# Key terms of three cross attentions made inside other stages, and two heads' keys loaded ahead of time

## What is computed

```python
q = (x @ Wq + bq).reshape(1, 1024, 16, 8)
k = (ctx_1024 @ Wk + bk).reshape(1, 6404, 16, 8)
v = (ctx_1024 @ Wv + bv).reshape(1, 6404, 16, 8)
attn = softmax(einsum('bthd,bshd->bhts', q, k) / sqrt(8), axis=-1)
out = einsum('bhts,bshd->bthd', attn, v).reshape(1, 1024, 128)
```

## Time and profile before

| | |
|---|---|
| Median of 3 runs | 4346.12 us (4341.44 to 4347.59) |
| Span of the profiled execution | 4349.1 us |
| TensorE busy | 3644.3 us, 84% |
| VectorE busy | 3405.6 us, 78% |
| ScalarE busy | 2821.1 us, 65% |
| GpSimd busy | 274.0 us, 6% |
| Score maxima on VectorE (L1666) | 2791.2 us in 2496 reductions |
| Exponentials on ScalarE (L1647) | 2452.8 us |

### The profile page before, as it was taken

The page is one execution under the profiler, slowest core; times in us unless marked ns, Lnnn a source line. Parts: engine busy times, 40 slices in busy tenths (PEclk is TensorE's granted clock), DMA queues, the critical chain, the costliest instruction groups (busy, mean ns, idle before and its releaser), DMA issues. The chain is left out here.

```text
span 4349.1 us, 85479 instructions
## 1 busy us (share of the span) xinstructions
PE 3644.3 (84%) x35064; PEld 1230.6 (28%) x35126; DVE 3405.6 (78%) x3306; ACT 2821.1 (65%) x4041; POOL 274.0 (6%) x199
## 2 busy tenths in 40 slices
PE   5774699999999747999999997399748999999995
PEld 2551222222222212222222222155312222222221
DVE  4323799999999328999999992499839999999982
ACT  0332288888888722888888886155415888888884
POOL 3001000000000010000000000244310000000000
PEclk9557599999999965999999999699857999999998
DMA  3003211111111031101111101100040111111100
GB/s 98 1 1 67 34 18 23 26 27 20 21 27 15 18 78 24 26 14 27 26 27 22 19 15 32 34 5 5 5 87 12 27 27 27 22 18 27 27 4 21
DMA packets 56289, 114.71 MB, mean 26 GB/s; under 512 B 10592, under 2 KB 46304, under 8 KB 50944
## 3 DMA queue, kind: packets, MB, share of 16 engines
q1 hardware_dynamic: 55936, 109.72, 14.1%
HBM read 84.08 MB, written 25.50 MB: 25 GB/s over the span
## 5 line engine op out<-in xcount | busy, mean ns | idle before, releaser
L1666 DVE TENSOR_REDUCE chunk_max<-max_scores 128x2 f32<-128x988 f32 (+1 forms) x2496 | 2791.2, 1179 | 193.4 <-PE max_scores L1549 158.2
L1647 ACT ACTIVATE probs<-scores 128x512 f32<-128x512 f32 (+1 forms) x3231 | 2452.8, 808 | 536.3 <-PE scores L1575 513.6
L1602 PE MATMUL values_sum<-probs,values 128*9 128x256 f32 x19584 | 1378.8, 384 | 26.7 <-DVE values_sum_s L1677 18.5
L1575 PE MATMUL scores<-queries,key_ring 49*128 49x512 bf16 x4800 | 1232.8, 386 | 50.9 <-ACT probs L1647 18.3
L1549 PE MATMUL max_scores<-key_ring,queries 48*128 48x494 bf16 (+1 forms) x4992 | 986.0, 393 | 157.6 <-DVE chunk_max L1666 113.1
L1602 PEld LDWEIGHTS values_sum<-probs,values 128*9 128x9 f32 x19584 | 376.8, 89 | 791.0 <-issue 569.2
L1575 PEld LDWEIGHTS scores<-queries,key_ring 49*128 49x128 bf16 x4800 | 308.1, 94 | 644.4 <-ACT probs L1647 542.3
L1549 PEld LDWEIGHTS max_scores<-key_ring,queries 48*128 48x128 bf16 x4992 | 241.0, 94 | 853.6 <-DVE chunk_max L1666 546.8
L1186 ACT ACTIVATE probs<-scores 128x512 f32<-128x512 f32 x256 | 138.5, 592 | 106.0 <-PE scores L1138 106.0
L1212 DVE TENSOR_REDUCE chunk_max<-max_scores 128x1024 f32 (+1 forms) x128 | 155.0, 1214 | 25.9 <-PE max_scores L1094 25.8
L1677 DVE COPY values_sum_s<-values_sum 128x256 f32<-128x256 f32 x48 | 20.0, 416 | 183.7 <-PE values_sum L1602 183.7
(11 more groups left out here) (183 smaller groups left out, 1742.5 us busy)
## 6 DMA issues: line engine op xcount, KB each, us to landing
key_ring<-k_parts SPq DMA_DIRECT2D x96, 300.2 KB
key_ring<-k_parts SPq DMA_DIRECT2D x96, 200.1 KB
k_parts<-k_part SPq DMA_DIRECT2D x108, 128.0 KB, 2.3
key_ring<-k_parts SPq DMA_DIRECT2D x96, 100.1 KB
o_whole<-values_sum_s SPq DMA_DIRECT2D x48, 128.0 KB, 7.0
queries<-q_parts SPq DMA_DIRECT2D x36, 128.0 KB
context<-in_ctx_t SPq DMA_DIRECT2D x1, 3202.0 KB, 17.2
q_parts<-q_part SPq DMA_DIRECT2D x12, 256.0 KB, 2.8
```

Of the source, the lines that this page charges most:

```text
L1575: return pe.matmul(sc[:, g % 3, :], keys(rows, h, P * t, P * (t + 1)), qb[rows, q], start=True, stop=True)
L1602: mm = pe.matmul(acc[32 * b:32 * b + WV, 0:QBLOCK], vb[rows, h, t, :], pr[rows, slot, QBLOCK * (b % 2):QBLOCK * (b % 2 + 1)], start=(t == ...
L1647: act.activation(pr[:, a % RING:a % RING + b - a, :], sc[:, a % 3:a % 3 + b - a, :], ACT.Exp)\
L1666: dve.tensor_reduce(mx[:, h % 2, c, :, j], mxb[:, w % 2, :, 0:width], AX.X, ALU.max)\
```

## The change

- `key_terms` is gone. The first cross attention's key terms are made in the first layer's value stage, now `project_values_and_keys`: before each of the first 13 value products stands a key product, with the same split and the same three slots. VectorE's sum over the context stands behind its key work.
- The key terms of the second and third cross attention are made in the tail of the one before (`ahead`): behind operation 1005 and every fourth after it TensorE makes one chunk's product into a bank of the score maxima; VectorE makes all three terms (four instructions a chunk) in the unused half of `queries`, with four slots, and SyncE stores them. Each cross attention has a `k_parts` of its own.
- The 12 fetches of query rows move to the end of `query_terms`, each group behind the store of its term.
- The keys of heads 0 and 1 are loaded ahead of `cross_attention`: beside `project_windowed` for the first, in a stage of their own (`load_first_keys`) behind the first cross attention for the second, and behind `clear_self_rows` of the self attention for the third (one ring place further, `base` = 1).
- The ones in the ring are filled once: 3072 columns by GpSimd and one row of each half from memory (`ones_row`, 9606 floats). What the self attention overwrites is filled again by GpSimd beside a layer norm.

```diff
--- before.py
+++ after.py
+def ring_keys(k, rows, h, base, lo=0, hi=M):
+    at = ((h + base) % KRING) * M
+    return k.key_ring[rows, at + lo:at + hi]
+
+def load_keys(k, sp, h, base, k_parts, loaded):
+    for half in range(2):
+        for p, run_length in enumerate(K_RUNS):
+            row = 64 * half + FIRST_ROW[p]
+            sp.dma_start(ring_keys(k, slice(row, row + HD * run_length), h, base),
+                         k_parts[h, 0:run_length].rearrange("p d n -> (p d) n")).then_inc(loaded, 16)
+
+def load_first_keys(k, layer, base, k_parts):
+    with ExitStack() as ctx:
+        block = ctx.enter_context(k.nc.Block())
+        @block.sync
+        def _(sp):
+            for h in range(2):
+                load_keys(k, sp, h, base, k_parts, k.first_keys[layer])
+
+def store_key_terms(sp, k_parts, part, c, slot, stored):
+    w = chunk_width(c)
+    for p in range(NPART):
+        sp.dma_start(k_parts[:, p, :, CHUNK * c:CHUNK * c + w], part[:, p, slot, 0:w]).then_inc(stored, 16)
+
-def project_values(k, xn, wv, vs, beside_vector):
+def project_values_and_keys(k, xn, wv, vs, wk, bk, k_parts, beside_vector):
...
+            def keys(c):
+                if c >= 4:
+                    pe.wait_ge(rest_ready, c - 3)
+                pe.matmul(kbank[c % 4][:, 0:chunk_width(c)], wk, k.ctx_t[:, CHUNK * c:CHUNK * c + chunk_width(c)],
+                          start=True, stop=True).then_inc(k_product, 1)
+
+            for g in range(NSEG):
+                if g < NCHUNK:
+                    keys(g)
+                values(g)
...
             for g in range(NSEG):
+                if g < NCHUNK:
+                    act.wait_ge(k_product, g + 1)
+                    if g >= 3:
+                        act.wait_ge(stored[g % 3], 16 * NPART * (g // 3))
+                    w = chunk_width(g)
+                    act.activation(part[:, 0, g % 3, 0:w], kbank[g % 4][:, 0:w], ACT.Identity, bias=bk).then_inc(high, 1)
                 act.wait_ge(projected, g + 1)
                 act.activation(vs[:, g, :], bank[g % 4][:], ACT.Copy).then_inc(copied, 1)
+                if g < NCHUNK:
+                    middle_part(g)
...
+            for c in range(NCHUNK):
+                dve.wait_ge(high, c + 1)
+                if c >= 3:
+                    dve.wait_ge(low, c - 2)
...
+                if c >= 1:
+                    low_part(c - 1)
+            low_part(NCHUNK - 1)
             beside_vector(dve)
...
-def project_windowed(k, w_o, o_pairs):
+def project_windowed(k, w_o, o_pairs, k_parts, ones_row):
...
+                pool.memset(k.key_ring[64 * half + 32:64 * half + 64, 0:KRING * N].bitcast(F32), PAIR_OF_ONES)\
+                    .then_inc(filled, 1)
...
+            sp.wait_ge(filled, 2)
+            for half in range(2):
+                row = 64 * half + KROWS
+                sp.dma_start(k.key_ring[row:row + 1, :].bitcast(F32), ones_row).then_inc(k.first_keys[0], 16)
+            for h in range(2):
+                load_keys(k, sp, h, 0, k_parts, k.first_keys[0])
...
@@ query_terms @@
             for p in range(NPART):
                 sp.wait_ge(stored[p], 16)
+                if rows_of is not None:
+                    for half in range(2):
+                        for r in range(K_RUNS[p]):
...
+            if rows_of is not None:
+                sp.wait_ge(fetched, 16 * 2 * NTERM)
...
-def key_terms(k, wk, bk, kb, qb, q_parts, k_parts):
...
+AHEAD_EVERY = 4
-def cross_attention(k, kb, qb, vb, k_parts, o_whole, wv):
+def cross_attention(k, layer, base, qb, vb, k_parts, o_whole, wv, ahead=None):
...
-            load_keys(0)
-            load_keys(1)
             max_rows(0)
...
+            if ahead is not None:
+                for c in range(NCHUNK):
+                    sp.wait_ge(next_low, c + 1)
+                    store_key_terms(sp, ahead[2], part, c, c % 4, next_stored[c % 4])
             store_values(H - 1)
...
+                if ahead is not None and n > tail_op and (n - tail_op) % AHEAD_EVERY == 1:
+                    next_key_product((n - tail_op) // AHEAD_EVERY)
...
+            def next_key_terms(c):
...
+                dve.wait_ge(next_product, c + 1)
+                if c >= 4:
+                    dve.wait_ge(next_stored[slot], 16 * NPART * (c // 4))
+                if bk is None:
+                    dve.tensor_copy(first, src).then_inc(next_high, 1)
...
             for h in range(H):
+                if h == H - 1 and ahead is not None:
+                    for c in range(NCHUNK):
+                        next_key_terms(c)
...
@@ program, attend @@
-                key_terms(k, k.w[prefix + w[1]], bk, kb, qb, q_parts, k_parts)
...
+            if layer == 0:
+                load_first_keys(k, 1, 0, k_parts[1])
             then()
...
             clear_self_rows(k, kb, qb)
+            load_first_keys(k, 2, 1, k_parts[2])
...
+            layer_norm(k, k.x[:], v["L3_xattn_ln2_g"], v["L3_xattn_ln2_b"], hn[:], t1[:], t2[:], beside=restore_ones(k))
```

More of the change, by code:

```diff
@@ L96, in __init__ @@
         self.steps = 0
+        self.first_keys = [ctx.enter_context(nc.semaphore(f"first_keys_{n}")) for n in range(3)]
     def name(self, text):
@@ L446, in _, with values @@
         def _(pe):
-            for g in range(NSEG):
+            def values(g):
                 if g >= 4:
@@ L466, in project_extra_values, with _ @@
+            low_part(NCHUNK - 1)
+            beside_vector(dve)
+        @block.sync
+        def _(sp):
+            for c in range(NCHUNK):
+                sp.wait_ge(high, c + 1)
+                sp.wait_ge(middle, c + 1)
+                sp.wait_ge(low, c + 1)
+                store_key_terms(sp, k_parts, part, c, c % 3, stored[c % 3])
+            for b in range(3):
+                sp.wait_ge(stored[b], 16 * NPART * len(range(b, NCHUNK, 3)))
 def project_extra_values(k, mem_tok, wv, vx):
@@ L798, in query_terms @@
         stored = [sem("stored") for _ in range(NPART)]
+        fetched = sem("fetched")
         block = open_phase(k, ctx)
@@ L1488, in cross_attention, with keys @@
         o_stored = [sem("o_stored") for _ in range(2)]
-        block = open_phase(k, ctx)
-        def keys(half, h, lo, hi):
-            at = (h % KRING) * M
-            return kb[half, at + lo:at + hi]
+        next_product = sem("next_product")
+        next_high = sem("next_high")
+        next_rest = sem("next_rest")
+        next_middle = sem("next_middle")
+        next_low = sem("next_low")
+        next_stored = [sem("next_stored") for _ in range(4)]
+        block = open_phase(k, ctx)
+        spare = qb[:, H * HALF:]
+        rest = spare[:, 0:4 * CHUNK].bitcast(F32).rearrange("p (s n) -> p s n", s=2)
+        part = spare[:, 4 * CHUNK:(4 + NPART * 4) * CHUNK].rearrange("p (t s n) -> p t s n", t=NPART, s=4)
+        tail_op = next(n for n in range(NOPS) if entries_through(n) == NENTRY)
+        def keys(rows, h, lo, hi):
+            return ring_keys(k, rows, h, base, lo, hi)
         @block.sync
         def _(sp):
-            def load_keys(h):
-                for half in range(2):
-                    for p, run_length in enumerate(K_RUNS):
-                        row = 64 * half + FIRST_ROW[p]
-                        sp.dma_start(keys(slice(row, row + HD * run_length), h, 0, M),
-                                     k_parts[h, 0:run_length].rearrange("p d n -> (p d) n"))\
-                          .then_inc(keys_loaded[h % KRING], 16)
             def max_rows(h):
@@ L1530, in _ @@
                 sp.wait_ge(o_stored[b], 16 * (H // 2))
+            if ahead is not None:
+                for b in range(4):
+                    sp.wait_ge(next_stored[b], 16 * NPART * len(range(b, NCHUNK, 4)))
         @block.tensor
@@ L1677, in take_values @@
                 dve.tensor_copy(acc_s[:, h % 2, :], acc[:, 0:QBLOCK]).then_inc(acc_taken, 1)
+            def next_key_terms(c):
+                wk, bk, _ = ahead
+                width, slot = chunk_width(c), c % 4
+                src = mxb[:, c // 2 % 2, c % 2, 0:width]
+                first, second, third = (part[:, t, slot, 0:width] for t in range(NPART))
+                left = rest[:, c % 2, 0:width]
+                dve.wait_ge(next_product, c + 1)
+                if c >= 4:
+                    dve.wait_ge(next_stored[slot], 16 * NPART * (c // 4))
+                if bk is None:
+                    dve.tensor_copy(first, src).then_inc(next_high, 1)
+                else:
+                    dve.tensor_scalar(first, src, bk, None, ALU.add).then_inc(next_high, 1)
+                dve.wait_ge(next_high, c + 1)
+                if bk is None:
+                    dve.tensor_tensor(left, src, first, ALU.subtract).then_inc(next_rest, 1)
+                else:
+                    dve.scalar_tensor_tensor(out=left, in0=src, scalar=bk, in1=first, op0=ALU.add, op1=ALU.subtract)\
+                       .then_inc(next_rest, 1)
+                dve.wait_ge(next_rest, c + 1)
```

(3 more changed lines are left out.)

179 lines of the change are left out of this document (74 added, 105 removed).

## The result

The changed kernel takes 4291.97 us (median of 4 runs, 4286.83 to 4306.88), the kernel before 4345.73 on the same chip: a ratio of 0.9886, 95% interval 0.9871 to 0.9902. The forecast of 4277 had the sign and the main mechanism right and was 15 us too low. The profiled execution took 4295.77 us, its span is 4294.0 us, 55.1 less than before.

What follows compares the result with a forecast made beforehand. Score maxima on VectorE and exponentials on ScalarE fill most of the span; the change works at the seams. 110 + 28.9 - 29 - 21.6 - 12 - 7 = 69.3 us won, so 4277 us, range 4250 to 4304.

Steps and rivals of the forecast that it cites:

- Key stages and first waits: Three seams before the cross attentions: removing key stages wins 110 us, removing TensorE's wait for first keys 28.9 us.
- My lower bound of 10 us for the fetch: Query-row fetch: at the keys' 164 GB/s it takes 10 us, not 25, and 45 us more are won.
- Value stage: First layer's value stage, now with key products: 46 us instead of 17.0, +29 us; bounds +11 and +52.
- The tails: Ends of the first two cross attentions: key products at 0.86 us, counted in full, 10.8 us per tail, 21.6 us together.
- The lower bound of 5.7 a tail: Cross attention tails: TensorE's idle 0.42 us in 3.30 covers part of each key product, leaving 0.44 us for each of 13.
- one of my signs of being wrong: Tails: any wait of TensorE on `next_rest` would show the forecast wrong.
- The early load of the second: Behind the first cross attention: weights and head sums queue behind keys, first reciprocal 12 us later; bounds 4.9 and 15.
- The early load of the third: Ahead of the self attention's query stage: keys in at 15 us, 19 us against 11.5, so +7, same bounds.
- The windowed part: Windowed projection and what follows: the first cross attention's early loads and GpSimd's fills beside it cost nothing.
- The clock: Rival: the clock stays up in the cross attentions' score maxima, gaining 30 us, so 4247; chance 0.08.
- The row of ones: Slower rival: two 9606-float DMAs delay the first query stores until 631, giving 4537; chance 0.04 with any stall like it.
- Every cost at its upper end: Rival: ScalarE's pause lost at each product (+8), early loads 15 each (+11), value stage's queues +6: 4302; chance 0.09.

Runs made afterwards that it cites:

- the kernel with all gains: Changed kernel plus both late key loads, four-buffer value stage with context sum in three pieces, all 13 value projections before the first maximum and fetch wait: 4198.92 us, ratio 0.9669.
- the kernel with the projections first: Changed kernel with the fetch wait moved to TensorE before its first maximum and all 13 groups of value projections ahead of it: 4244.66 us, ratio 0.9768.

## Why the prediction was right, and where it missed

- **Key stages and first waits.** Right: 138.9 us forecast, 143.5 measured. The fetch alone was taken as 25 us, and 1 us more for its start, which no row shows by itself; with its wait moved to TensorE it is in 27 us after its issue (405.03 to 432.2 with three groups of projections ahead, 399.80 to 427.1 in the kernel with all gains), and the stages began 32.5, 26.7 and 29.6 us after the first store, where I had 31.2 for each. My lower bound of 10 us for the fetch rested on the keys' rate, which was wrong (below).
- **Value stage.** Right to 2 us: chunk 3 started 10.7 us into the stage (11.3), the low terms ended at 40.0 (38.7), the stage at 48.0 (46). That the sum stood alone on the path was nearly wrong: without it the last stores would have held the stage until 1.2 us before the same end.
- **The tails.** A little mis-sized: a tail grew by 9.4 us instead of 10.8. The records give the granted clock as a share of full speed and no frequency, so where the prediction and an expectation name one, only the share is shown: it is 1.00 (window 378.60 to 379.10 us) at the pass of 0.43 us, and 0.50 (376.40 to 377.20 us) at an earlier one of the same stage, which takes 0.34 + 0.52 = 0.86 us (kernel before, timeline of TensorE's weight loads):

```profile
377.23 0.34 PEld L1344 LDWEIGHTS k_product<-context,squares 128*128 128x128 f32 x1 [0.52 <-issue]
```

  "I therefore count it in full", 0.86 us a product, holds for neither part of the tail: the first four cost 1.05, so part of ScalarE's pause is lost with them, the rest cost 0.62, so TensorE's idle time covers some. The lower bound of 5.7 a tail is not reached at any place (6.9 at best). In the second tail TensorE waited at most 0.9 us in all for `next_rest`, one of my signs of being wrong, at no cost that the tail shows (71.4 us in both). The bodies ahead of the tails became 2.7 and 4.4 us shorter. In the second, 1.9 of the 4.4 lie ahead of the first head's negative maximum, where the granted clock was 0.67, 0.61 and 0.56 in three of six windows of 10 us, against 0.50 in all six before; for the rest I have no cause.
- **The early load of the second.** The step that failed: "Keys took 451.46 - 436.43 = 15.0 us to land". That row ends when the first head's keys are in; the wait in the code (`keys_loaded[h % KRING]`) is for one head's six loads. I divided two heads' bytes by one head's time, 164 GB/s instead of about 100. At the right rate the 2.46 MB are in some 25 us after 1508.6, and all that is queued behind comes later: the first reciprocal was 26.1 us late, not 12, and outside my bounds of 4.9 and 15. The stretch cost 16.3 us more than forecast. An estimate from these rows: 10.6 of them are the keys' time (25.6 instead of 15.0), some 3 are a load that started 0.6 us later and weights and sums that took 4.9 us behind the keys instead of 2.5, and 2.2 lie behind the reciprocal. These last are no price of the load, since the kernel that loads late has them too. The runs with and without the load, and with one or two heads waited for, show the rest.
- **The early load of the third.** The same step: 15.3 us instead of 7. In the self attention's query stage (timeline of SyncE, changed kernel):

```profile
2733.66 4.40 SPq L404 DMA_DIRECT2D key_ring<-k_parts  x12
2743.90 2.63 SPq L950 DMA_DIRECT2D q_parts<-q_part  x3
...
2761.81 6.30 SPq L1013 DMA_DIRECT2D queries<-q_parts  x6
```

  From the first key issue to the fetch in the next stage are 28.2 us where I had 19, and from the query stores to that fetch 17.9, against 8.1 in the kernel before and 8.2 with the load placed late. Loading late gave back 16.6.
- **The windowed part.** Forecast at nothing, measured +3.7. In the kernels with the change this stretch takes either 240 to 242 or about 246 us (242.8 before), with the same instructions in it, so this is no price of the ones row; what makes the difference is open.
- **The rivals.** The clock did not stay up: in the window 451 to 461 us it is at 0.50, TensorE 7.25 of 10 us busy, waiting for VectorE between its pairs of products. So it was right not to give this rival more than 0.08. The row of ones cost nothing that can be seen: its two issues took 0.62 us from 349.56 on, and the first query store behind it, issued at 402.24, had landed when the fetches began at 405.02. "Every cost at its upper end" gave 4302, nearer to 4292 than the forecast, but of its three parts only the early loads came (24.6 us above the forecast, where it had 11). One wrong rate moved two terms at once, and bounds from the same row shared the mistake.
- **The total.** That it came within 15 us is in part luck: 24.6 us missed at the early loads were partly made up by 4.6 us at the seams and 9.9 us between the first maxima and the last sums, most of which the forecast had no reason for.

## What to carry to other kernels

When a wait gives the duration of a transfer, read in the code which semaphore, and so how many bytes, it stands for. Queue an early load behind every small load on which the next step rests: here 2.46 MB ahead of eight head sums cost 26 us, behind them nothing. And when a stage that covered a transfer is removed, move work that doesn't need its data under it: the change of stage and the value projections, moved there, were worth 47 us, against 54 for the whole change.

## What the runs showed of the hardware

- The twelve fetches of query rows did not fill the DMA engines in any window read. From 1590 to 1600 us, in the changed kernel, with nothing else in the queue (window, columns as in the earlier trace rows):

```profile
1590.00:1600.00 10.00, 0.00 (x0) 0.00 (x0) 0.00 (x0) 0.00 (x0) 0.00 (x0) 0.50 0.56 81
```

  The share was 0.57 at 66 and 65 GB/s in the two windows of the kernel with the projections first. The same column reads up to 1.13 where all is taken, so it can't be read more finely. No run here fetched in another shape, so what keeps the share there is not shown.
- One issue of a load of 128 KB took SyncE 9.85 us behind the twelve key loads, against 0.6 where the keys stood behind it. What held it is not shown; three query stores behind twelve other key loads were issued in their usual 2.63 us.
- The seam with the same fetch, from the first store to the next stage, took between 26.6 and 32.5 us, from seam to seam and execution to execution of kernels with the same code there. That, and the stretch of 240 or 246 us, is noise of some microseconds which one profile does not show.
